# Combine weights' transposes and first bias product half a step earlier, first parts half a step later, last chunk's x and bias add inside attention

## What is computed

```python
h = layernorm(x)
q, k, v = h @ Wq.T + bq, h @ Wk.T + bk, h @ Wv.T + bv    # 16 heads of 16
q, k = rope(q), rope(k)
x = x + softmax(q k^T / 4) v @ Wo.T + bo
h = layernorm(x)
xc = bf16(h)
normed = bf16(xc * rsqrt(mean(xc^2) + eps) * norm_weight)
logits = normed @ gate_weight.T                          # 8 experts
combine = softmax weights of the two largest logits, 0 elsewhere
g, lin = min(p1[0::2], 7), clip(p1[1::2], -7, 7)         # p1 = normed @ mlp1_e.T + b1_e
act_e = g * sigmoid(1.702 g) * (lin + 1)
out = x + xc + bf16(sum over e of combine_e * (act_e @ mlp2_e.T + b2_e))
```

## Time and profile before

| | |
|---|---|
| median of 3 runs | 1063.61 us (1063.59 to 1067.9) |
| the profiled execution | 1064.35 us, of which the span from first to last instruction is 1062.5 us |
| busy, share of the span | PE 88%, DVE 72%, ACT 71%, POOL 38%, PE's weight loads 38% |
| mean granted TensorE clock | 0.961 |
| DMA | 109.76 MB, mean 103 GB/s |

### The profile page before, as it was taken

How to read it: one execution, slowest core, us unless ns; L and a number is a source line. 1 busy time by engine, 2 the same in 40 slices (tenths; PEclk the granted TensorE clock), 3 DMA queues, 4 the chain that set the end, 5 groups by cost and what they waited for, 6 DMA issues and landing times. The chain is left out here.

```text
span 1062.5 us, 16544 instructions
## 1 busy us (share of the span) xinstructions
PE 935.2 (88%) x5217; PEld 398.7 (38%) x5288; DVE 765.6 (72%) x1514; ACT 750.6 (71%) x1018; POOL 406.1 (38%) x341
## 2 busy tenths in 40 slices
PE   5669898999988999989989999889998999998496
PEld 3312222244332444334342444334442444344364
DVE  5851202689858886679858888688867786779797
ACT  1458895867867687767768677787878887885252
POOL 3525205352365325534263533652332324143310
PEclk9869998999999999989999999999999999999699
DMA  5264473325535343445534245344544453513121
GB/s 170 89 160 105 96 142 83 86 81 131 126 66 142 96 113 98 108 106 131 124 72 115 81 111 131 87 119 120 116 100 99 114 127 85 117 52 104 35 61 35
DMA packets 79984, 109.76 MB, mean 103 GB/s; under 512 B 22530, under 2 KB 56722, under 8 KB 76818
## 3 DMA queue, kind: packets, MB, share of 16 engines
q1 hardware_dynamic: 61460, 83.47, 33.4%
q10 hardware_dynamic: 18432, 25.17, 8.3%
HBM read 82.90 MB, written 25.69 MB: 102 GB/s over the span
## 5 line engine op out<-in xcount | busy, mean ns | idle before, releaser
L877 ACT ACTIVATE probs<-S 128x1024 f32<-128x1024 f32 x512 | 513.0, 1024 | 144.4 <-PE S L726 143.0
L726 PE MATMUL S<-Qs,Ks 98*128 98x512 bf16 x1024 | 301.8, 388 | 21.4 <-ACT probs L877 18.2
L740 PE MATMUL OP<-probs,V 128*17 128x512 f32 x2048 | 275.5, 610 | 3.6 <-ACT O L886 3.6
L964 POOL TENSOR_TENSOR act_lo<-act_sb,act_hi 128x512 fp32r<-128x512 f32 x112 | 152.5, 1363 | 134.0 <-ACT act_hi L866 133.7
L726 PEld LDWEIGHTS S<-Qs,Ks 98*128 98x128 bf16 x1024 | 79.4, 99 | 200.6 <-ACT probs L877 97.6
L712 PE MATMUL D<-W,act_hi 128*128 128x256 f32 x448 | 130.7, 324 | 13.4 <-DVE acc L1183 3.6
L1183 DVE SCALAR_TENSOR_TENSOR acc<-D,combh,acc 128x256 f32<-128x256 f32 x224 | 97.3, 475 | 55.0 <-PE D L712 54.6
L958 POOL TENSOR_SCALAR W<-W2b 128x512 fp32r<-128x512 bf16 x64 | 41.5, 649 | 222.4 <-PE D L712 177.2
L1191 DVE SCALAR_TENSOR_TENSOR th_sb<-th_sb,g_sb 128x512 f32<-128x512 f32 x112 | 107.3, 958 | 14.4 <-ACT th_sb L853 10.7
L712 PE MATMUL D<-W,act_lo 128*128 128x256 f32 x448 | 112.1, 282 | 0.0
L712 PEld LDWEIGHTS D<-W,act_hi 128*128 128x128 f32 x448 | 85.1, 190 | 39.2 <-DVE nsq L1045 6.8
(11 more groups left out here) (172 smaller groups left out, 1014.4 us busy)
## 6 DMA issues: line engine op xcount, KB each, us to landing
W<-in_w ACTq DMA_DIRECT2D x64, 256.0 KB, 2.8
Ks<-k_scr SPq DMA_DIRECT2D x32, 384.0 KB
W2b<-in_w ACTq DMA_DIRECT2D x64, 128.0 KB, 2.9
Ks<-k_scr SPq DMA_DIRECT2D x32, 256.0 KB
o_scr<-O SPq DMA_DIRECT2D x32, 256.0 KB, 4.7
Qs<-q_scr SPq DMA_DIRECT2D x32, 192.0 KB
k_scr<-parts SPq DMA_DIRECT2D x12, 384.0 KB, 3.3
q_scr<-parts SPq DMA_DIRECT2D x12, 384.0 KB, 3.4
```

The source lines that it names most:

```text
L726: last = mm(S[:, j2, C * i:C * (i + 1)], Ks[0:SROWS + MROWS, g % 2, j, P * kt:P * (kt + 1)], Qs[0:SROWS + MROWS, g % 2, j, :], start=True, ...
L740: last = mm(OP[32 * j:32 * j + VW, :], V[:, kt, HG * g + j, :], probs[:, s % 2, C * j:C * (j + 1)], start=kt == 0, stop=kt == KT - 1)
L877: nc.scalar.activation(probs[:, s % 2, 2 * C * j2:2 * C * (j2 + 1)], S[:, j2, :], ACT.Exp, scale=SCALE).then_inc(exp_done, 1)
L964: tt(act_lo[:, e % 2, it, :], act_sb[:, a % 2, :], act_hi[:, e % 2, it, :].bitcast(FP32), ALU.subtract).then_inc(lo_s, 1)
```

## The change

Three numbers of the table AT change: `part1` stands four halves behind its `qk` instead of three, so ScalarE's cast and square of all tiles of chunks 0 to 5 are one half step later (halves 14, 16, 26 and 34), while GpSimd's, VectorE's and TensorE's parts of `length` stay at five. `combT` moves from half 32 to 31 and `b20` from 33 to 32; `b21` stays at 34. They move in chunks 1 to 7 and in the tail.

For chunk 7 alone, the load of its x moves from the tail's half 0 to half 43 of its own attention, and GpSimd's bias add from the tail's half 11 to half 55. And in the tail, the reciprocal is taken at the second place of step 2 instead of the first place of step 3, ahead of the stages there.

```diff
-          "qk3": 30, "rope": 2, "part1": 3, "length": 5, "part2": 7, "part3": 10, "v0": 37, "v1": 42, "gmax": 1,
+          "qk3": 30, "rope": 2, "part1": 4, "length": 5, "part2": 7, "part3": 10, "v0": 37, "v1": 42, "gmax": 1,
...
-          "combT": 32, "b20": 33, "b21": 34}
+          "combT": 31, "b20": 32, "b21": 34}
...
+    LAST_IN, POST_END = {}, {k: [e for e in l if e[0] not in ("x1_in", "x1_b")] for k, l in POST.items()}
+    for st, h in (("x1_in", 43), ("x1_b", 55)):
+        place(LAST_IN, h, (st, 0))
...
             if post:
-                todo += [(st, a, before) for st, a in POST.get((step, place), [])]
+                todo += [(st, a, before) for st, a in (POST_END if b is B else POST).get((step, place), [])]
                 todo += [(st, a, before) for st, a in EXPERTS.get((step, place), [])]
+            if b is B - 1 and n == NCH - 1:
+                todo += [(st, a, (b, n)) for st, a in LAST_IN.get((step, place), [])]
...
-                    if kt == 3 and not first and place in (None, 0):
+                    if (kt, place) in ((3, None), (2, 1)) and not first:
                         dve.wait_ge(sum_r, 64 * (G + 1))
                         v.reciprocal(rec_c[:, :], sums_c[:, :]).then_inc(rec_s, 1)
```

## The result

The changed kernel takes 1054.39 us (median of 4 runs, 1050.43 to 1055.87), the kernel before took 1065.4 us beside it on the same chip (1063.59 to 1067.9): a ratio of 0.9889 [0.985, 0.9929]. The forecast was 1048.5 us, from 1041 to 1060. The profiled execution took 1055.73 us with a span of 1053.9, which is 8.6 less than the 1062.5 of before.

A forecast was written before the change was run, and what follows sets the result against it. TensorE, busy 88%, was taken as the bound, with in-order queues bounding the combine-weight stretches and its clock falling behind them. Terms 9.4 + 1.5 + 1.6 + 2.3 + 1.0 - 3.1 + 3.2 = 15.9 off 1064.35 gave 1048.5 us, range 1041 to 1060.

The forecast's parts named there:

- the forecast's own signs of being wrong: Length products showing waits of a microsecond, or the clock row having as many slices below 9 as before.
- A: Combine-weight stretches, chunks 1 to 5: TensorE's clock falls go with the wait before the second bias product; 9.4 us.
- B: Rest of those stretches: the reduction freeing the V product's bank comes 0.3 us earlier in five chunks; 1.5 us.
- C: Chunk 0's tiles: an exponential runs in ScalarE's idle time ahead of the cast; 1.6 us.
- D: Chunk 1's first tile: exponential goes ahead of cast and square, value products start at 181.8; 2.3 us.
- E: Chunks 6 and 7, without tiles: the second bias product's 0.52 us wait goes; 1.0 us.
- F: Last chunk's bias add at half 55 holds VectorE's hidden product 2.15 us and adds one clock fall; -3.1 us.
- G: Tail: reciprocal 1.3 us earlier, projection at full clock, second x1 add 3.4 us earlier; 3.2 us taken.
- the second: Small gains don't carry, as VectorE's gate chain sets the next step; 1054.9 us, chance 0.12.
- The first rival: Falls stay: waits shift to the first bias product and the length product; 1057.9 us, chance 0.15.
- The third: More falls go: chunk 1 loses two and the bias add sets off none; 1043.7 us, chance 0.15.
- The fourth: Slower: length products wait for cast and square in all 24 tiles, 30 us; 1078.5 us, chance 0.05.

The follow-up runs named there:

- filled: Kernel before, with TensorE computing two score products three times over in step 17 of chunks 1 to 5, where it would wait; 1059.14 us, 0.9944.
- part1_only: Kernel before with only the tiles' cast and square half a step later; 1064.08 us, 0.9994.
- tail_only: Kernel before with only the end's edits: last chunk's x load and bias add inside its attention, earlier reciprocal; 1061.8 us, 0.9968.
- after2: The changed kernel measured again, unaltered, in a second set of runs; 1054.03 us, 0.9911.
- b21_33: Changed kernel with the second bias product half a step earlier too (half 33); 1059.87 us, 0.9961.
- x1_wait: Changed kernel with GpSimd holding the last chunk's bias add until VectorE's hidden product is done; 1052.49 us, 0.9874.
- x1_back: Changed kernel with last chunk's x load and bias add back in the tail, reciprocal kept early; 1052.29 us, 0.9888.
- recip_back: Changed kernel with the tail's reciprocal at its old place; 1056.15 us, 0.9916.

## Why the prediction came out as it did

The direction and the order of size were right, the sum was 4 to 6 us too high (15.9 against 11.8 and 9.5 by the two ratios). One of the forecast's own signs of being wrong came true: a length product does wait over a microsecond (1.33 and 1.16 us); the other, the clock row, did not. The chances named for "faster" add up to 0.875, not 0.85. By parts, in the profiled executions:

**A, the clock: 9.4 forecast, 7.4 seen, 6.0 for all falls in a typical execution.** The mechanism stands: the wait before the second bias product brings the falls. Filling it takes them all away (`filled`), leaving it in place keeps them (`part1_only`). The step that failed is the size: "the price of the falls is the excess over chunk 5" was read from one execution. Of the waits of 1.65 us and more in three kernels that have them, 10 of 15 met a fall: 4, 4 and 2 of 5 (before, `part1_only`, `tail_only`), worth 9.1, 6.1 and 3.1 us in the stretches of steps 16 to 19. Their mean is 6.1, beside the 6.0 of `filled`. Of the 45 waits of 1.30 to 1.34 us in the nine traces that have those, 3 met one. That the falls would go was in part luck: I took them as gone because the new waits would be under half as long, and the one at the length product is four fifths of the old one. The Trainium skill (TensorE: Matmul & The Clock Gate, "What's actually happening") calls the monitor free-running; that the same wait in chunk 4 of the changed kernel meets a fall in one execution and not in `after2` agrees with it. `part1_only`'s two groups of times, some 7 us apart with different mean clocks, may be the same thing.

**B, the rest of these stretches: 1.5 forecast, 0.3 seen** (5 x 0.06). The step that failed is "0.4 before the next length product". I had checked that product against its square and not against the bank it shares: the copy of the second bias product came behind the hidden product and two evacuations, and it waits 1.33 us. From there to the V product TensorE stands idle nowhere, so this wait took the place of the old one as the bound. `b21_33` shows what stands close behind it: the reduction (L1052), late when the hidden product ahead of it meets GpSimd's low part. Neither move gives anything here at full clock: 17.17 and 16.53 us each alone, 16.47 together.

**C, chunk 0: 1.6 forecast, 0.7 in this profile.** Steps 7 to 19 give 1.7. A longer stretch of half clock at the chunk's start, where nothing was changed, took 1.1 back (steps 1 to 4); `after2` has 84.2 us against 85.7, `x1_wait` 83.9. Right.

**D, chunk 1: 2.3 forecast, 0.9 seen.** The step itself was right to 0.05 us (181.75). What it ran into is the wait of 2.55 us behind the norm's squares and the fall behind it: the next five steps gave back 2.1 of 3.0 us. `part1_only` has the same wait (2.56 us), no fall behind it, and gains 2.8 up to step 16. Every kernel with both moves has a fall there, without a cause that these runs show; in `after2` it is a longer one, and the chunk is 0.5 us slower up to step 16 than before.

**E, chunks 6 and 7: 1.0 forecast, 0.5 seen** (12.84 to 12.61 in each; the wait of the earlier trace rows is gone), and chunk 6 gave 0.3 of it back at step 23, for which I have no cause.

**F, the bias add: -3.1 forecast, -1.4 seen.** The block was right: the hidden product took 2.74 us for 0.69, 2.05 late (forecast 2.15), and steps 28 and 29 grew by 1.4 (forecast 1.5). The fall that I added to it didn't come: TensorE had its down products between and waited 1.27 us, not 2.3. The Trainium skill (SBUF — State Buffer, "Who interferes with whom") has this exclusion, and the rows agree: the hidden product ends 0.55 us behind the add, nearly its 0.69 alone, as if begun when that ended. In all fourteen traces every hidden product of over 1.5 us ends 0.54 or 0.55 us behind a GpSimd operation. `x1_wait` removes it and `x1_back` shows that the move as made earns nothing.

**G, the tail: 3.2 forecast, 1.4 seen** (2.2 in `after2`; the five traces without these edits have tails of 98.0 us in the mean, the four of the changed kernel and `x1_wait` 95.6). The reciprocal's 1.3 us came, of which `recip_back` shows 0.6 at the x1 add, and the projection ran at once and at full clock (1.89 us, where the earlier trace rows had 0.50). Two steps failed. The x1 add was to follow the projection directly; but VectorE's hidden product met GpSimd's low part, took 1.64 us, and put the add at 2.6 us earlier instead of 3.4. And "the norms and gates behind it [...] move with it" held (2.6 at the gates), but the first down product of chunk 7 fell mostly into a stretch at half clock, 2.79 us where it had taken 1.89, so 0.9 of the 2.3 us by which it started earlier were lost. It took 1.93 in `after2`.

**The rivals.** The time is that of the second, 1054.9, and in part for its reason: B didn't carry, D and E carried less than half, and C gave its sum in its own steps. That the number fits is luck beyond that: A and G, which this rival left alone, came out 2.0 and 1.8 us short in the profile, and F, 1.7 us better than forecast, made up for one of them. And its named cause, VectorE's gate chain, is not what the runs show. The first rival was right that waits would move to the length product, and wrong in what follows: 3 of 45 met a fall. The third had one thing right, that the bias add sets off none. The fourth foresaw waits of the length product; they are 6.3 us in ten waits for the square and 6.6 in five for the bank, not 30, and the stretches of both moves don't grow by them (16.47 us against 16.53).

**What stays open.** Step 7 of chunks 6 and 7 takes 4.6 to 5.4 us in most traces and 6.6 to 7.9 in one of them in five (`after2`, `tail_only`, `recip_back`, `part1_only`, `b21_33`), which blurs differences of 2 us between single profiles. In these five, and in no other step 7 of the two chunks, the hidden product takes 2.73 us beside the bias add of that chunk, as in part F: in `after2` the add starts at 771.13 and the hidden product at 771.76, while in the changed kernel's first trace the add comes 1.1 us behind it (773.92, 772.85) and the step takes 4.79. Why the add comes earlier in some executions is open, and holding it there as `x1_wait` does was not tried. Why a wait of 1.33 us meets far fewer falls than one of 1.66 was seen and not explained.

## What to carry to other kernels

When a product is moved ahead in a shared bank, check the next user of that bank and not the moved one alone: the wait goes to whoever fills it next, behind the same slow instruction. Look at what the move does to the meetings of VectorE's and GpSimd's operations too: 0.7 us a stretch hung on a hidden product that met a low part or just escaped it. Price a loss of clock over several executions, or by a kernel that fills the wait with spare work, before it goes into a sum; one profile gave 9.4 us for what is worth 6. And measure two moves together before dropping one: here they gave 4.4 and 0.6 alone and 9.0 as a pair, and of the 4.0 between the traces account for 3.5.

## What the runs showed of the hardware

- Six spare products in a wait of 1.66 us made the kernel 6.0 us faster with nothing else changed (`filled`). Filler on the engine that is busiest can pay.
- Executions of one kernel differ by up to 12 us (1058.84 to 1070.94 for the kernel before in one set of runs), and in `part1_only` the longer ones are those with the lower mean clock.
- VectorE's hidden product takes 0.69 us alone, 1.64 beside a GpSimd operation of 1.3, and 2.74 beside one of 2.3, while GpSimd's own takes 2.81 instead of 2.34. Whenever it takes over 1.5 us it ends 0.54 or 0.55 us behind a GpSimd operation, in all fourteen traces. VectorE's copy out of PSUM took no longer than usual (0.67) beside GpSimd's subtraction L948.
- Eight float32 passes of a down product (L707, L714) take 1.89 us at full clock and 2.90 at a clock of 0.65 (`x1_back`), and the tail's length follows this one product to 0.04 us in fourteen traces.
